# A GNN with mixture-of-experts layer on one Trainium2 core: more edges in the dense chunks, four late pairs, experts' weights loaded one expert at a time

## Chip, cores and metric

The kernel runs on one core of a Trainium2 chip. The metric is the device time of one execution in microseconds (us). The program is scheduled by hand: each engine (PE, the TensorE; DVE, the VectorE; ACT, the ScalarE; POOL, the GpSimd; SP, the SyncE, which here only issues DMAs) has its own instruction stream, and semaphores order them.

## What is computed

The input x has 6250 nodes of 256 features, with 206,250 edges sorted by target node. The reference, cut down:

```python
def gcn_layer(x, W, b):
    msg = (x @ W)[src] * norm[:, None]
    return relu(segment_sum(msg, dst, num_segments=6250) + b)

norm = edge_weight * rsqrt(deg_out[src] * deg_in[dst] + 1e-12)
h = gcn_layer(gcn_layer(layernorm(x), W6, b6), W7, b7)
x = x + h @ Wp + bp

xn = layernorm(layernorm(x)) * gamma + beta
top_vals, top_idx = top_k(xn @ Wr + br, 2)
w = softmax(top_vals)
for e in range(8):
    y += (gelu(xn @ W1[e] + b1[e]) @ W2[e] + b2[e]) * w_full[:, e]
x = x + y
```

Each expert has a W1 of 256 x 512 and a W2 of 512 x 256, float32.

## The kernel before

**Edges.** The edges form 202 groups of 8 tiles of 128 edges. They are summed in two ways. A *sparse* group is gathered: POOL issues 8 indirect DMAs (`gathers`, L912), each of which fetches 128 table rows; PE adds them per target node with 16 matmuls (`sums`, L2012) and one more (`combine`, L2024); ACT copies the sums out (`copy_sums` L1670, `copy_rows` L1677), and SP stores them to `zsum` in DRAM (`store_group`, L708). The ring of gathered groups has four places, so that POOL waits for the sums of the fourth group back. A *dense* tile is not gathered. DVE writes two one-hot matrices for it (`tile_one_hots`, L1218 and L1219), PE turns them into a piece of an adjacency matrix with three bf16 matmuls (`build_tile`, L1979), and DVE adds that to the adjacency of its chunk (`add_tile`, L1238). A *chunk* of `CT` = 30 tiles is then applied to the whole feature table in 27 steps of 98 matmuls in all (`apply_step`, L1992). The first 90 groups are dense in layer 1 (24 chunks, 720 tiles); two extra chunks of `LATE_CT` = 24 tiles make it 96 groups in layer 2.

**Layer 1.** A loop of 12 turns handles two chunks and 8 sparse groups in each: while PE builds the tiles of one chunk it applies the chunk before. SP stores each finished chunk to DRAM, for layer 2. After the loop a tail of `TAIL` = 16 turns sums the last 16 groups, builds the extra chunks (`EXTRAS`) and projects the pairs: a *pair* is 256 nodes, 25 in all, 23 of which come two or three a turn from turn 4 on (`TAIL_PAIRS`). For a pair SP loads its sums (`load_early`, which calls `load_pair`, L734, into `zrow`), DVE scales them (L1275), PE transposes them (L2033), ACT applies bias and relu (`pair_relu`, L1710, into `hT`), and PE projects them (L2050). The result is the feature table of layer 2, without which POOL can't gather there.

**Layer 2** runs in slots, one per sparse group. A chunk takes `SPANS[c]` slots: three for the first `SHORT` = 6, then four. On the first slot of a chunk SP issues the load of the chunk after it (`load_chunk`, L728). Each pair passes six stages in six successive slots: 0 scales, transposes and projects it; 1 adds the residual (DVE, L1287) and normalizes twice; 2 transposes (L2063) and takes the router's logits (L2073); 3 ranks the experts and adds the second bias, for which ACT copies eight weights per node (L1742) and PE multiplies (L2094), and SP stores the pair's rows (`rows_x`, L766) and its accumulator (`acc`, `store_acc`, L770); 4 and 5 place it in the experts' lists (one-hots by DVE, L1373; PE, L2112). `pair_from` says from which slot on a pair's sums are ready, and `pair_starts` makes the table `STARTS` from it, pairs at least three slots apart. The residual of a pair uses the same buffer as the accumulator store of the pair before. At the slot after the last chunk (`CHUNKS_END` = 98) ACT issues the loads of all experts' weights (`load_experts`, `load_weights`, L1817 and L1818): their place in SBUF is that of layer 1's table, free once the last chunk is applied.

**Experts.** From slot `GROUPS[1]` on, two blocks of 128 (token, expert) places run per slot, 105 in all. POOL gathers a block's rows (`take_block`, L923), PE and ACT run the two matmuls and gelu, ACT weights the result (`block_out`, L1797), and POOL adds it to `acc` in DRAM by an indirect DMA (`add_block`, L936). Blocks under `WHOLE` = 74 are formed from the lists of the first 22 pairs alone and their adds may go two in flight; from `WHOLE` on, where the `LATE_PAIRS` = 3 last started pairs come in, each add waits for the one before.

Of the kernel before, what the change touches and what calls it, by code (L numbers as in the profile page):

```python
# [6 lines left out]
BF16 = mybir.dt.bfloat16  # L7
# [35 lines left out]
GROUP_AT = [CT * h + 7 * s + 4 for h in range(2) for s in range(GPI // 2)]  # L43
# [8 lines left out]
BLOCKS, LATE_PAIRS, ZERO_PAIRS, PER_SLOT = 105, 3, 2, 2  # L52
# [29 lines left out]
def gnn_moe_kernel(nc, A):  # L82
# [36 lines left out]
    with ExitStack() as ctx:  # L119
# [43 lines left out]
        iota_b = sb("iota_b", [P, P], BF16)  # L163
# [7 lines left out]
        iota_col = sb("iota_col", [P, PLACES], BF16)  # L171
# [94 lines left out]
        col_n = area(o_a + 2 * P + KEYS, PLACES).bitcast(I32)  # L266
# [54 lines left out]
        trash = l2(PT)  # L321

# [111 lines left out]
        x_stored, hot_ready, list_mm = sem("x_stored"), sem("hot_ready"), sem("list_mm")  # L434
        list_closed, list_copied, last_row_made = sem("list_closed"), sem("list_copied"), sem("last_row_made")
# [77 lines left out]
        def chunk_slot(it, u):  # L513

            return 2 * it - 1 + u // CT, u % CT


        STEPS = CT - 3
# [6 lines left out]
        def group_at(it):  # L525

            return GROUP_AT if it else FIRST_GROUPS_AT

        def slice_bounds(i):
# [4 lines left out]
        TURNS = TAIL - TAIL_FROM - 2  # L534
        TAIL_PAIRS = [range(0)] * TAIL_FROM + [range(LATE_PAIR * k // TURNS, LATE_PAIR * (k + 1) // TURNS)
                                               for k in range(TURNS)] + [range(0)] * 2
# [14 lines left out]
        def chunk_start(c):  # L551
            return CT * min(c, CHUNKS) + LATE_CT * max(c - CHUNKS, 0)

        def chunk_of(t):
            return t // CT if t < DT else CHUNKS + (t - DT) // LATE_CT
# [5 lines left out]
        EXTRAS = [range(DT + LATE_CT * k // FIRST_EXTRA, DT + LATE_CT * (k + 1) // FIRST_EXTRA)  # L561
                  for k in range(FIRST_EXTRA)]
        EXTRAS += [range(DTA - LATE_CT + LATE_CT * k // 8, DTA - LATE_CT + LATE_CT * (k + 1) // 8) for k in range(8)]
# [21 lines left out]
        def chunks_for(b):  # L585
            return next(c for c in range(ALL) if chunk_start(c) >= tiles_before((b + 1) * PT * P) + CT // 2)
# [35 lines left out]
        assert [b for _, b in STARTS[-LATE_PAIRS:]] == [*MERGED_PAIRS, NPAIR - 2, NPAIR - 1]  # L622
        assert CHUNKS_END < LISTED_AT and COPIED_AT < GROUPS[1] and WHOLE % 2 == 0
# [29 lines left out]
        def _(sp):  # L653
# [108 lines left out]
            def store_x(i, b, slot):  # L762

                sp.wait_ge(wf_ready, i + 1)
                sp.wait_ge(rows_zeroed, 16 * 2 * PT * ZERO_PAIRS)
                sp.dma_start(pair_rows(rows_x, b), zx[:, slot]).then_inc(x_stored, 16)  # L766
# [6 lines left out]
            with sp.If(bad < 1):  # L773
# [6 lines left out]
                for it in range(LOOP_GROUPS // GPI):  # L780
                    for u in range(2 * CT):
# [114 lines left out]
        def _(pool):  # L896
# [3 lines left out]
            pool.iota(col_n, pattern=[[1, PLACES]], base=-(PLACES // 2), channel_multiplier=0).then_inc(iota_made, 1)  # L900
# [74 lines left out]
        def _(dve):  # L975
# [25 lines left out]
            dve.wait_ge(iota_made, 5)  # L1001
            dve.tensor_copy(iota_f[:, :], iota_i)
            dve.tensor_copy(iota_b[:, :], iota_i)
            dve.tensor_copy(iota_key[:, 0:KEYS], key_i)
            dve.tensor_copy(iota_col[:, :], col_n)
# [138 lines left out]
            spans = (0, DT, 0, CHUNKS, CT), (DT, DTA, CHUNKS, ALL, LATE_CT)  # L1144
# [5 lines left out]
            for q in range(QUARTERS):  # L1150
# [5 lines left out]
            dve.tensor_tensor(cseld[:, 1:CHUNKS + 1], tmin_f[:, CT:DT + CT:CT], tmin_f[:, 0:DT:CT], ALU.subtract)  # L1156
            step(dve.tensor_tensor(cseld[:, CHUNKS + 1:], tmin_f[:, DT + LATE_CT:DTA:LATE_CT],
                                   tmin_f[:, DT:DTA - LATE_CT:LATE_CT], ALU.subtract))
# [217 lines left out]

            def copy_list():
# [180 lines left out]
            with dve.If(bad < 1):  # L1558
# [5 lines left out]
                for it in range(LOOP_GROUPS // GPI):  # L1564
                    for u in range(2 * CT):
                        t = it * 2 * CT + u
# [19 lines left out]
                for k in range(TAIL):  # L1586
# [18 lines left out]
            with dve.Else():  # L1605
# [10 lines left out]
                slow_layer(1)  # L1616
                with dve.Fori(0, NPAIR - LATE_PAIRS) as b:
# [27 lines left out]
        def _(act):  # L1645
# [220 lines left out]
            with act.If(bad < 1):  # L1866
# [3 lines left out]
                for it in range(LOOP_GROUPS // GPI):  # L1870
                    for u in range(2 * CT):
# [10 lines left out]
                for k in range(TAIL):  # L1882
# [8 lines left out]
                    if k == FIRST_STORED_AT:  # L1891
                        act.wait_ge(added, DT + LATE_CT)
# [12 lines left out]
            with act.Else():  # L1905
# [19 lines left out]
                load_weights()  # L1925
# [19 lines left out]
        def _(pe):  # L1945
# [151 lines left out]
            def open_list():  # L2097
                pe.matmul(ps_list, no_part, iota_col[0:1, :], start=True, stop=False)
# [139 lines left out]
            with pe.If(bad < 1):  # L2238
                for t in range(len(ps_b)):
                    build_tile(t)  # L2240
                for it in range(LOOP_GROUPS // GPI):
                    for u in range(2 * CT):
                        t = it * 2 * CT + u
                        c, step = chunk_slot(it, u)
                        if c >= 0 and step < STEPS:
                            if step == 0:
                                pe.wait_ge(added, CT * (c + 1))
# [131 lines left out]
```

## Time and profile before

| | us |
|---|---|
| median of 3 runs | 3206.28 |
| lowest and highest run | 3199.44, 3208.09 |
| the profiled execution | 3203.64 |
| span of its trace | 3201.8 |
| PE busy | 2693.6 (84%) |
| POOL busy | 1988.3 (62%) |
| DVE busy | 1897.6 (59%) |
| ACT busy | 854.6 (27%) |

The mean granted clock of the profiled execution is 0.926 of full speed. In the trace, times count from the span's start; "idle ... <-X" or "[... <-X]" is the time the engine stood before an instruction, and what ended that time. "issue" means that it waited for nothing the trace shows. Layer 1's gathers start at 373.5 us; layer 2's run from 1573.67 to 2668; the experts' blocks end at 3170.7.

### The profile page before, as it was taken

What the parts mean: (1) busy time and instruction counts of PE and PEld (TensorE: products, weight loads), DVE (VectorE), ACT (ScalarE), POOL (GpSimd) and SP (SyncE); (2) the same over time, 40 slices, a digit from 0 to 9 for tenths busy, and PEclk for the clock granted to TensorE, in tenths of its full rate; (3) what the DMA queues carried; (4) which work ended last, traced back from release to release, by engine and by line L of the source; (5) the groups of instructions that cost most, each with busy time, mean ns of one, the idle gap of its engine ahead of it and who ended that gap; (6) DMA issues with size and microseconds to landing.
All of it is one profiled execution on the core that took longest, in us unless ns stands there. A gap on an engine that the chain in (4) does not pass through costs nothing. (4 is left out here: it accounts for less than half of the span.)

```text
span 3201.8 us, 53454 instructions
## 1 busy us (share of the span) xinstructions
PE 2693.6 (84%) x17249; PEld 2025.2 (63%) x17249; DVE 1897.6 (59%) x5981; ACT 854.6 (27%) x2004; POOL 1988.3 (62%) x1964
## 2 busy tenths in 40 slices
PE   4567489999999999987599999999888876899984
PEld 3456257666666666654477666666666643789974
DVE  9999878887878878764204445555354446622210
ACT  5677611111111111113200101111000001456542
POOL 0000277777777777777477777777777663467653
PEclk8699799999999999998899999999998885999997
DMA  4011355555655555558667667666766663344434
GB/s 127 0 30 34 119 189 191 191 187 178 196 196 195 195 195 193 195 165 279 219 200 259 223 221 228 217 219 225 234 194 198 211 225 82 65 68 70 73 56 112
DMA packets 196686, 532.68 MB, mean 166 GB/s; under 512 B 39708, under 2 KB 127412, under 8 KB 189652
## 3 DMA queue, kind: packets, MB, share of 16 engines
q0 software_dynamic: 103872, 256.67, 31.0%
q1 hardware_dynamic: 89828, 254.39, 21.8%
q10 hardware_dynamic: 2736, 18.48, 1.5%
q8 instruction: 133, 2.18, 0.3%
q14 instruction: 117, 0.96, 0.1%
HBM read 379.28 MB, written 156.50 MB: 167 GB/s over the span
## 5 line engine op out<-in xcount | busy, mean ns | idle before, releaser
L912 POOL DMA_INDIRECT arena<-table,src_i x1744 | 1699.1, 974 | 598.5 <-issue 526.4
L1992 PE MATMUL bank<-arena 128*128 128x257 f32 x4900 | 1238.6, 388 | 4.5 <-ACT zcd L1689 3.7
L1992 PEld LDWEIGHTS bank<-arena 128*128 128x128 f32 x4900 | 885.7, 192 | 217.8 <-issue 106.7
L1238 DVE TENSOR_TENSOR arena<-arena,bank 128x294 f32 x768 | 348.9, 454 | 227.5 <-PE bank L1979 154.9
L1979 PE MATMUL bank<-arena 128*128 128x294 bf16 x2304 | 418.3, 295 | 71.1 <-DVE arena L1238 37.7
L1979 PEld LDWEIGHTS bank<-arena 128*128 128x128 bf16 x2304 | 222.4, 99 | 227.9 <-DVE arena L1238 64.5
L1219 DVE SCALAR_TENSOR_TENSOR arena<-iota_f,arena 128x256 f32<-128x256 f32 x768 | 359.8, 469 | 0.0
L2012 PE MATMUL bank<-arena,s_all 128*32 128x257 f32 x3488 | 299.1, 412 | 46.7 <-DMA arena<-table,src_i 41.1
L936 POOL DMA_INDIRECT acc<-arena x105 | 179.5, 1709 | 155.6 <-ACT arena L1797 130.8
L1680 ACT COPY arena<-zero 128x2144 f32<-128x2144 f32 (+1 forms) x104 | 159.1, 1561 | 381.7 <-DMA chunks<-arena 248.7
L1951 PE MATMUL bank<-arena 128*128 128x150 bf16 x1616 | 149.0, 252 | 111.4 <-DVE arena L1068 75.8
L1670 ACT COPY zs<-bank 128x257 f32<-128x257 f32 x109 | 40.9, 375 | 738.8 <-PE bank L2012 738.8
L1218 DVE TENSOR_SCALAR arena<-iota_key,arena 128x294 bf16<-128x294 bf16 x768 | 235.1, 306 | 0.0
L1490 DVE COPY arena<-arena 128x1024 f32 x105 | 75.7, 729 | 268.0 <-PE bank L2197 254.2
L903 POOL PARTITION_ALL_REDUCE bad_all<-bad_f x1 | 0.4, 380 | 358.2 <-DVE bad_f L1209 358.2
L2206 PE MATMUL bank<-arena 128*128 x840 | 203.1, 384 | 17.4 <-ACT arena L1797 17.4
L1951 PEld LDWEIGHTS bank<-arena 128*128 128x128 bf16 x1616 | 129.6, 108 | 132.2 <-DVE arena L1068 110.7
L2012 PEld LDWEIGHTS bank<-arena,s_all 128*32 128x32 f32 x3488 | 122.0, 114 | 142.3 <-issue 50.8
L2197 PE MATMUL bank<-arena 128*128 128x128 f32 x1680 | 208.5, 278 | 0.0
L2197 PEld LDWEIGHTS bank<-arena 128*128 128x128 f32 x1680 | 199.9, 195 | 0.1
L2206 PEld LDWEIGHTS bank<-arena 128*128 128x128 f32 x840 | 152.0, 191 | 39.1 <-issue 21.5
L923 POOL DMA_INDIRECT arena<-rows_x,arena x105 | 108.0, 1028 | 65.9 <-DVE arena L1400 35.7
(241 smaller groups left out, 2780.1 us busy)
## 6 DMA issues: line engine op xcount, KB each, us to landing
chunks<-arena SPq DMA_DIRECT2D x25, 3283.0 KB
arena<-chunks SPq DMA_DIRECT2D x24, 3283.0 KB, 13.4
arena<-table,src_i POOLq DMA_INDIRECT x1744
zsum<-zc SPq DMA_DIRECT2D x109, 128.5 KB, 3.6
zrow<-zsum SPq DMA_DIRECT2D x50, 257.0 KB, 4.6
arena<-in_W ACTq DMA_DIRECT2D x16, 512.0 KB, 16.4
rows_x<-arena SPq DMA_DIRECT2D x25, 264.0 KB
arena<-chunks ACTq DMA_DIRECT2D x2, 3283.0 KB, 13.2
```

Source lines behind the costliest of these rows:

```text
L912: pool.indirect_dma_start(gat[:, r, j, 0:D], None, table[L], bass.IndirectOffsetOnAxis(ap=src_i[:, col:col + 1], axis=0)).then_inc(gathere ...
L936: pool.indirect_dma_start(acc, bass.IndirectOffsetOnAxis(ap=row_e[:, j:j + 1], axis=0), ye[:, j % 2], None, compute_op=ALU.add).then_inc(y ...
L1218: dve.tensor_scalar(ohk[:, r], iota_key[:, 0:KEYS], key[:, t:t + 1], None, ALU.is_equal)
L1219: dve.scalar_tensor_tensor(out=words[:, r], in0=bc_mid(iota_f[:, :], 2), scalar=lo_f[:, t:t + 1], in1=bc_in(w_words[:, t], P), op0=ALU.is_ ...
L1238: dve.tensor_tensor(win, win, ps_b[t % len(ps_b)].rearrange("p (h w) -> p h w", w=TW), ALU.add).then_inc(added, 1)
L1680: act.copy(adj[:, c % 2, first:last], zero[:, :].unsqueeze(2).broadcast_to([P, last - first, AWID])).then_inc(zeroed, 1)
L1951: last = pe.matmul(ps_do, oh_lo[:, r, j // TI, :, j % TI], whi[:, r, j // TI, :, :, j % TI].rearrange("p i n -> p (i n)"), start=False, st ...
L1979: last = pe.matmul(ps_b[t % len(ps_b)], halves[:, t % OH_RING, word, :, half], ohk[:, t % OH_RING], start=(i == 0), stop=(i == 2))
L1992: last = pe.matmul(ps_ap, adj[:, c % 2, h, 0:P], xp[:, h], start=(h == 0), stop=(h == XB_ALL - 1))
L2012: last = pe.matmul(ps_seg[q * WIN:(q + 1) * WIN, :], s_mat[:, r, q * HQ + j], gat[:, r, q * HQ + j], start=(j == 0 and not second), stop=( ...
L2197: last = pe.matmul(ps_h[j % 2][:, c], w1_e[:, j % W1_RING, k, c * P:(c + 1) * P], xeT[:, j % 2, k], start=(k == 0), stop=(k == KD - 1))
L2206: last = pe.matmul(ps_y, hs[:, j % 2, c], w2_of(e, c), start=(c == 0), stop=(c == HC - 1))
```

## The change

- The chunks' sizes become a list: 16 chunks of 31 tiles, 8 of 30, then extra chunks of 17 and 31 (before: 24 of 30, and 24, 24). Dense tiles in layer 1: 736 in place of 720; in layer 2: 784 in place of 768. So two groups fewer are gathered in each layer (110 and 104 in place of 112 and 106), and the tail has 14 turns in place of 16.
- Eight chunks of layer 2 take three slots in place of six; `CHUNKS_END` falls from 98 to 96, and the slots from 115 to 113.
- The four last started pairs are late in place of three: `WHOLE` falls from 74 to 70, and SP writes zeros to the rows of four pairs at the start (16 DMAs) in place of two (8).
- The weights are loaded one expert per slot in the eight slots from `CHUNKS_END` on, two DMAs each, in place of 16 at once.
- `iota_b` and `iota_col`, constants of the list, are made late in layer 1's tail (`list_constants`) in place of the start, and lie where other data is dead by then.

```diff
-CT = 30
-DT = CHUNKS * CT
-LATE_CHUNKS, LATE_CT, SHORT = 2, 24, 6
-ALL = CHUNKS + LATE_CHUNKS
-DTA = DT + LATE_CHUNKS * LATE_CT
+SIZES = [31] * 16 + [30] * 8 + [17, 31]
+ALL, SHORT = len(SIZES), 8
+DT, DTA = sum(SIZES[:CHUNKS]), sum(SIZES)
...
-BLOCKS, LATE_PAIRS, ZERO_PAIRS, PER_SLOT = 105, 3, 2, 2
+BLOCKS, LATE_PAIRS, PER_SLOT = 105, 4, 2
...
-        TURNS = TAIL - TAIL_FROM - 2
+        TURNS = TAIL - TAIL_FROM - 1
...
-            for t in range(NB - ZERO_PAIRS * PT, NB):
+            for t in [b * PT + t for _, b in STARTS[-LATE_PAIRS:] for t in range(PT)]:
...
+            def list_constants():
+                dve.tensor_copy(iota_b, iota_f[:, :])
+                for at in range(0, PLACES, P):
+                    n = min(P, PLACES - at)
+                    last = dve.tensor_scalar(iota_col[:, at:at + n], iota_f[:, 0:n], float(at - PLACES // 2), None, ALU.add)
+                last.then_inc(columns_made, 1)
...
+                    if k == TAIL - 2:
+                        list_constants()
...
                 if n == CHUNKS_END:
-                    load_experts()
+                    act.wait_ge(applied[1], SLICES * ALL)
+                if CHUNKS_END <= n < CHUNKS_END + NE:
+                    load_expert(n - CHUNKS_END)
...
-            def load_experts():
-                act.wait_ge(applied[1], SLICES * ALL)
-                load_weights()
-
-            def load_weights():
-                for e in range(NE):
-                    act.dma_start(w1_sb[:, e], A["W1"][:, e * KD * H:(e + 1) * KD * H]).then_inc(w1_in, 16)
-                    act.dma_start(w2_sb[:, e], A["W2"][:, e * HC * D:(e + 1) * HC * D]).then_inc(w2_in, 16)
+            def load_expert(e):
+                act.dma_start(w1_sb[:, e], A["W1"][:, e * KD * H:(e + 1) * KD * H]).then_inc(w1_in, 16)
+                act.dma_start(w2_sb[:, e], A["W2"][:, e * HC * D:(e + 1) * HC * D]).then_inc(w2_in, 16)
```

The table `STARTS`, slots in which the pairs start, comes out so: before 10, 14, 17, 22, 27, 32, 35, 40, 43, 48, 51, 56, 59, 64, 71, 74, 79, 82, 87, 90, 95, 98, 101, 106, 109; now 10, 13, 16, 20, 23, 30, 33, 38, 41, 46, 49, 54, 57, 62, 65, 70, 73, 78, 85, 88, 93, 96, 99, 104, 107. Chunks of four slots start on slots 18, 22, ... 94 before, on 24, 28, ... 92 now.

ACT, around the slot after the last chunk, before (`arena<-in_W` is a load of weights, the `COPY` of 8x256 the one for the second bias):

```order
L1731 ACTIVATE arena<-bank,cols 128x256 x2
L1677 COPY zc<-bank 128x257
L1737 ACTIVATE arena<-arena 128x2
L1817 DMA arena<-in_W 128x1024
L1818 DMA arena<-in_W 128x1024
...
L1818 DMA arena<-in_W 128x1024
L1742 COPY arena<-bank 8x256
L1710 ACTIVATE hT<-bank,cols 128x256 x2
```

and in the changed kernel:

```order
L1746 ACTIVATE arena<-bank,cols 128x256 x2
L1692 COPY zc<-bank 128x257
L1752 ACTIVATE arena<-arena 128x2
L1829 DMA arena<-in_W 128x1024
L1830 DMA arena<-in_W 128x1024
L1757 COPY arena<-bank 8x256
L1725 ACTIVATE hT<-bank,cols 128x256 x2
L1829 DMA arena<-in_W 128x1024
L1830 DMA arena<-in_W 128x1024
L1685 COPY zs<-bank 128x257
```

Sixteen loads stood ahead of the copy; now two do, and the others lie one pair a slot behind it.

SP in layer 2, before, at slot 74, where a chunk starts (`arena<-chunks` is the load of the next), a pair starts (`zrow`, `in_x`) and the pair of slot 71 is in stage 3 (`rows_x`, `acc`):

```order
L734 DMA zrow<-zsum 128x2x257
L760 DMA arena<-in_x 128x2x256
L711 TENSOR_LOAD bc_i
L711 ISA x2
L719 ISA
L719 DMA zsum<-zcd 128x257
L728 DMA arena<-chunks 128x6566
L766 DMA rows_x<-arena 128x2x264
L770 DMA acc<-arena 128x2x256
```

and in the changed kernel at slots 72 and 73, where the chunk and the pair start in turn:

```order
L723 DMA zsum<-zcd 128x257
L732 DMA arena<-chunks 128x6566
L738 DMA zrow<-zsum 128x2x257
L764 DMA arena<-in_x 128x2x256
L709 TENSOR_LOAD bg_i
L709 ISA x2
L712 ISA
L712 DMA zsum<-zc 128x257
L770 DMA rows_x<-arena 128x2x264
L774 DMA acc<-arena 128x2x256
```

The chunk's load moved from just ahead of the `acc` store to a slot ahead of it.

## Rows read from the trace of the kernel before

**Rows 1.** Costliest groups of the page: busy, mean ns of one, idle before.

```profile
L912 POOL DMA_INDIRECT arena<-table,src_i x1744 | 1699.1, 974 | 598.5 <-issue 526.4
...
L1979 PE MATMUL bank<-arena 128*128 128x294 bf16 x2304 | 418.3, 295 | 71.1 <-DVE arena L1238 37.7
```

**Rows 2.** Windows: PE, PEld, DVE, ACT, POOL busy, clock, DMA share, GB/s; dense loop.

```profile
560.00:720.00 160.00, 155.58 (x1016) 110.57 (x1013) 129.71 (x389) 30.83 (x36) 122.47 (x123) 1.00 0.59 189
```

**Rows 3.** Groups by line of PE from 415 to 1385, the dense loop.

```profile
L2012 PE MATMUL bank<-arena,s_all 128*32 128x257 f32 x1488 | 118.7, 388 | 17.5 <-DMA arena<-table,src_i 17.5
```

**Rows 4.** Timeline of POOL between the layers: start, duration, idle before.

```profile
1534.95 0.94 POOL L912 DMA_INDIRECT arena<-table,src_i  x1 [0.30 <-issue]
1573.67 0.94 POOL L912 DMA_INDIRECT arena<-table,src_i  x1 [37.78 <-DMA table<-arena]
```

**Rows 5.** Timeline of PE in layer 1's tail.

```profile
1461.50 2.86 PE L1979 MATMUL bank<-arena 128*128 128x294 bf16 x9 [6.31 <-DVE arena L1238]
...
1480.47 1.99 PE L2050 MATMUL bank<-w,hT 128*128 128x256 f32 x8 [0.93 <-ACT hT L1710]
...
1490.78 1.11 PE L2033 MATMUL bank<-ident,zr_all 128*128 128x128 f32 x4 [8.32 <-DVE zr_all L1275]
```

**Rows 6.** Windows of line L2012 alone, layer 2: PE, PEld, clock, DMA.

```profile
2060.00:2330.00 270.00, 38.12 (x448) 15.53 (x448) 0.95 0.71 226
2330.00:2610.00 280.00, 37.18 (x400) 14.79 (x400) 0.91 0.62 193
```

**Rows 7.** POOL late in layer 2: groups from 2470 to 2610; one timeline row.

```profile
L912 POOL DMA_INDIRECT arena<-table,src_i x102 | 97.1, 952 | 43.8 <-issue 29.8 <-PE bank L2012 14.0
...
2637.59 0.94 POOL L912 DMA_INDIRECT arena<-table,src_i  x1 [13.99 <-PE bank L2012]
```

**Rows 8.** Timeline of DVE, the residuals of pairs (L1287) in layer 2.

```profile
2047.75 0.69 DVE L1287 TENSOR_TENSOR arena<-bank,arena 128x512 f32<-128x512 f32 x1 [4.88 <-DMA acc<-arena]
...
2360.78 0.69 DVE L1287 TENSOR_TENSOR arena<-bank,arena 128x512 f32<-128x512 f32 x1 [11.10 <-DMA acc<-arena]
...
2540.73 0.69 DVE L1287 TENSOR_TENSOR arena<-bank,arena 128x512 f32<-128x512 f32 x1 [7.50 <-DMA acc<-arena]
```

**Rows 9.** Timeline of PE early in layer 2: apply matmuls back to back.

```profile
1719.57 4.95 PE L1992 MATMUL bank<-arena 128*128 128x257 f32 x22
```

**Rows 10.** Timeline of ACT and its queue at the weights' loads.

```profile
2607.71 0.36 ACTq L1817 DMA_DIRECT2D arena<-in_W  x1
...
2622.93 2.18 ACTq L1818 DMA_DIRECT2D arena<-in_W  x1
2625.21 0.36 ACT L1742 COPY arena<-bank 8x256 f32<-8x256 f32 x1 [17.31 <-issue]
```

**Rows 11.** Timeline of PE behind it.

```profile
2625.62 2.07 PE L2094 MATMUL bank<-arena 8*128 8x256 f32 x4 [15.33 <-ACT arena L1742]
...
2631.04 3.78 PE L2050 MATMUL bank<-arena,hT 128*128 128x256 f32 x8 [0.93 <-ACT hT L1710]
```

**Rows 12.** Windows ahead of the weights' loads and while they land (columns as in rows 2).

```profile
2560.00:2607.00 47.00, 44.97 (x266) 33.67 (x269) 22.92 (x101) 4.82 (x13) 33.16 (x35) 0.94 0.49 128
2617.00:2626.00 9.00, 0.38 (x1) 0.38 (x2) 0.00 (x0) 0.36 (x1) 5.08 (x6) 0.50 1.04 387
```

**Rows 13.** Timeline of ACT in the expert stage, ends of two blocks each.

```profile
2943.16 0.47 ACT L1797 ACTIVATE arena<-bank,arena 128x256 f32<-128x256 f32 x1 [0.58 <-PE bank L2206]
...
2946.91 0.48 ACT L1797 ACTIVATE arena<-bank,arena 128x256 f32<-128x256 f32 x1 [0.59 <-PE bank L2206]
...
3079.94 0.48 ACT L1797 ACTIVATE arena<-bank,arena 128x256 f32<-128x256 f32 x1 [2.65 <-DMA acc<-arena]
...
3084.56 0.48 ACT L1797 ACTIVATE arena<-bank,arena 128x256 f32<-128x256 f32 x1 [2.41 <-DMA acc<-arena]
```

More of the change, by code:

```diff
@@ L42 @@
 LOOP_GROUPS = 96
-GROUP_AT = [CT * h + 7 * s + 4 for h in range(2) for s in range(GPI // 2)]
+GROUP_AT = [7 * s + 4 for s in range(GPI // 2)]
 FIRST_GROUPS_AT = [5 * s + 18 for s in range(GPI)]
@@ L513, in chunk_slot, with tile_slots @@
         def chunk_slot(it, u):
-            return 2 * it - 1 + u // CT, u % CT
-        STEPS = CT - 3
+            first = SIZES[2 * it]
+            return (2 * it - 1, u) if u < first else (2 * it, u - first)
+        def tile_slots(it):
+            return range(SIZES[2 * it] + SIZES[2 * it + 1])
+        STEPS = 27
         ZERO_BEHIND = (8, 17, 25, STEPS - 1)
@@ L525, in group_at @@
         def group_at(it):
-            return GROUP_AT if it else FIRST_GROUPS_AT
+            return GROUP_AT + [SIZES[2 * it] + u for u in GROUP_AT] if it else FIRST_GROUPS_AT
         def slice_bounds(i):
@@ L551, in chunk_start @@
         def chunk_start(c):
-            return CT * min(c, CHUNKS) + LATE_CT * max(c - CHUNKS, 0)
+            return sum(SIZES[:c])
         def chunk_of(t):
-            return t // CT if t < DT else CHUNKS + (t - DT) // LATE_CT
+            return next(c for c in range(ALL) if t < chunk_start(c + 1))
         def group_no(L, n):
@@ L585, in chunks_for @@
         def chunks_for(b):
-            return next(c for c in range(ALL) if chunk_start(c) >= tiles_before((b + 1) * PT * P) + CT // 2)
+            return next(c for c in range(ALL) if chunk_start(c) >= tiles_before((b + 1) * PT * P) + 15)
         def groups_for(L, b):
@@ L621, in gnn_moe_kernel @@
         COPIED_AT = LISTED_AT + 3
-        assert [b for _, b in STARTS[-LATE_PAIRS:]] == [*MERGED_PAIRS, NPAIR - 2, NPAIR - 1]
-        assert CHUNKS_END < LISTED_AT and COPIED_AT < GROUPS[1] and WHOLE % 2 == 0
+        assert [b for _, b in STARTS[-LATE_PAIRS:]] == [NPAIR - 3, *MERGED_PAIRS, NPAIR - 2, NPAIR - 1]
+        assert CHUNKS_END <= LISTED_AT and CHUNKS_END + NE <= GROUPS[1] and COPIED_AT < GROUPS[1] and WHOLE % 2 == 0
         assert STARTS[-LATE_PAIRS][0] + 4 > COPIED_AT - 1
@@ L780, in _ @@
                 for it in range(LOOP_GROUPS // GPI):
-                    for u in range(2 * CT):
+                    for u in tile_slots(it):
                         c, step = chunk_slot(it, u)
@@ L1143, in _ @@
             dve.tensor_scalar(bg_i[:, :], tmin_f[:, ::2 * TG], float(ZROWS - P), None, ALU.min)
-            spans = (0, DT, 0, CHUNKS, CT), (DT, DTA, CHUNKS, ALL, LATE_CT)
+            turns = [c for c in range(ALL + 1) if c in (0, ALL) or SIZES[c] != SIZES[c - 1]]
+            spans = [(chunk_start(c0), chunk_start(c1), c0, c1, SIZES[c0]) for c0, c1 in zip(turns, turns[1:])]
             for t0, t1, c0, c1, n in spans:
@@ L1155, in _ @@
             dve.tensor_tensor(csel[:, 1:], tmin_f[:, 2 * TG::2 * TG], tmin_f[:, 0:-2 * TG:2 * TG], ALU.subtract)
-            dve.tensor_tensor(cseld[:, 1:CHUNKS + 1], tmin_f[:, CT:DT + CT:CT], tmin_f[:, 0:DT:CT], ALU.subtract)
-            step(dve.tensor_tensor(cseld[:, CHUNKS + 1:], tmin_f[:, DT + LATE_CT:DTA:LATE_CT],
-                                   tmin_f[:, DT:DTA - LATE_CT:LATE_CT], ALU.subtract))
+            for t0, t1, c0, c1, n in spans:
+                more = min(c1, ALL - 1) - c0
+                if more:
+                    last = dve.tensor_tensor(cseld[:, c0 + 1:c0 + more + 1], tmin_f[:, t0 + n:t0 + n * more + 1:n],
+                                             tmin_f[:, t0:t0 + n * more:n], ALU.subtract)
+            step(last)
             dve.tensor_scalar(off_i[:, :], dif[:, 0:DTA], 0.0, float(P), ALU.max, ALU.min)
@@ L1564, in _ @@
                 for it in range(LOOP_GROUPS // GPI):
-                    for u in range(2 * CT):
-                        t = it * 2 * CT + u
+                    for u in tile_slots(it):
+                        t = chunk_start(2 * it) + u
                         if t % LOADED == 0:
@@ L1616, in _ @@
                 slow_layer(1)
+                list_constants()
                 with dve.Fori(0, NPAIR - LATE_PAIRS) as b:
@@ L1870, in _ @@
                 for it in range(LOOP_GROUPS // GPI):
-                    for u in range(2 * CT):
+                    for u in tile_slots(it):
                         c, step = chunk_slot(it, u)
@@ L1924, in _ @@
                 act.wait_ge(p_stored, 16 * NPAIR)
-                load_weights()
+                for e in range(NE):
+                    load_expert(e)
                 with act.Fori(0, NPAIR) as b:
@@ L2241, in _ @@
                 for it in range(LOOP_GROUPS // GPI):
-                    for u in range(2 * CT):
-                        t = it * 2 * CT + u
+                    for u in tile_slots(it):
+                        t = chunk_start(2 * it) + u
                         c, step = chunk_slot(it, u)
```

26 lines of the change are left out of this document (13 added, 13 removed).

## The prediction

> **What bounds the kernel now.** I read the page first: its costliest group is POOL's gather, 1744 indirect DMAs with 1699.1 us busy, and all but 72 us of POOL's idle time before them is "issue" [rows 1]. The windows of the dense loop come next: in 160 us POOL starts 123 gathers, so 1.30 us each and 10.4 us for a group of 8, while PE is busy for 155.58 us of the 160 and DVE for 129.71 [rows 2]. Two engines are full at once there: PE waits for gathers only 17.5 us in 970 us of the loop [rows 3]. So shorter POOL work alone buys little, nor does shorter PE work. Third, the timeline of POOL: its last gather of layer 1 starts at 1534.95, the first of layer 2 at 1573.67, 38 us later [rows 4]. What fills these 38 us is the projection of the pairs: PE's timeline there shows it waiting for DVE (6.31 and 8.32 us) while POOL gathers on [rows 5]. In layer 2 the groups' sums (16 matmuls a group, one group a slot) tell which engine paces: 448/16 = 28 groups in 270 us is 9.6 us each, POOL's pace; 400/16 = 25 in the next 280 us is 11.2 us each, slower than POOL can go [rows 6]. PE paces from about 2330 on, and the waits of POOL for PE in [rows 7] agree.
>
> **The change, part by part.** *Sixteen tiles more in the chunks.* Two groups, 16 gathers, leave each layer. A tile costs PE three matmuls of 0.295 us [rows 1], 0.9 us: 16 x 0.9 = 14 us in layer 1. All sixteen lie in the loop, where PE's waits for gathers, 17.5 us, take them up; POOL still needs its 41.6 us for the four groups of a chunk. DVE has 30 us of 160 free [rows 2]. I take 0; if the waits don't come at the right chunks, up to +8. The two extra chunks stay 48 tiles together (17 and 31). Eight more zero fills at the start and the list's two constants, remade by five small DVE operations ahead of the last pairs, lie under other work: 0.
>
> *Layer 1's end.* POOL ends 16 x 1.30 = 20.8 us sooner. But the 23 pairs start once the last loop chunk is applied and cost PE 1.99 us of projection, 1.1 of transposes and 0.93 of waiting each [rows 5]; no gather of the group behind them is waited for there. The tail has two groups fewer to sum, about 2 x 1.7 us of PE work. I take -3, with ends 0 (pairs alone end the layer) and -21 (POOL does).
>
> *Layer 2.* 16 gathers of 1.25 us go: -20. From 2470 to 2610 POOL further waits 14.0 us for PE [rows 7]. Their cause, as I read it: where a pair starts three slots behind another on a chunk's first slot, SP issues the 3.3 MB chunk load just ahead of the acc store of the older pair, and DVE's residual of the younger one waits for that store, 11.10 us at the first and 7.50 at the last of three such places, against 4.88 where no load is ahead [rows 8]. In the new table of starts this falls on one slot (88) in place of three (74, 82, 90), so two thirds of the 14 us go: -9. Against it, slots 10 to 25 get fuller: five pairs start there (10, 13, 16, 20, 23) in place of four (10, 14, 17, 22), and chunks 6 and 7 have 3 slots in place of 4. A chunk of 98 apply matmuls at 4.95/22 us [rows 9] is 22 us of PE work; with three groups' sums (some 5 us) and one pair's (some 6 us) that is 33 us against POOL's 30. Over the five pairs that is 15 us of lag more, of which the ring of four groups (40 us of gathers) absorbs a part: +8, with ends 0 and +29 (all of it, at both places). Together -21, between -45 and +10.
>
> *The experts' weights.* Before, ACT issues all 16 loads of 512 KB in one go at slot 98, from 2607.71 to 2625.11. Its next copy waits 17.31 us, "issue" [rows 10], and PE, which needs that copy, stands for 15.33 us; its projection afterwards takes 3.78 us in place of 1.99 [rows 5, 11]. While PE stood, its granted clock was 0.50, the lower of its two levels (1.2 GHz), and the DMA engines were full, 387 GB/s [rows 12]. The change issues two loads in each of eight slots. Two take under 1 us where the queue is free (0.36 us for the first) [rows 10], and ACT is busy 4.82 us of 47 there [rows 12], so this hides. The transfers add 1.05 MB per 11 us, 95 GB/s, to the 128 that move in that stretch [rows 12]. I take -15.3 - 1.8 = -17, with ends 0 and -18. The row that speaks against the cover is POOL's wait for PE of 13.99 us at 2637.59 [rows 7]: it is the same stall, so not counted again. The Trainium skill ("DMA: Bandwidth & Descriptors", section "Issuing engines are not separate DMA queues") says that all issuers' DMAs run on the same 16 engines and interleave, and that the time to issue one "is usually small relative to the DMA itself". By it the stall would be the transfers' and spreading would save only the issue; the rows differ on the second half, since here issuing took 17.4 us of sequencer time that nothing could overtake, though the full engines are there too.
>
> *The expert stage.* WHOLE falls from 74 to 70: four more blocks whose scatter-add waits for the one before. Blocks with adds in pairs come 3.75 us apart (2943.16, 2946.91), serialized ones 4.62 (3079.94, 3084.56), with ACT waiting 2.4 us for the add [rows 13]: 4 x 0.87 = +3.5.
>
> **Sum:** 0 - 3 - 21 - 17 + 3.5 = -37.5. The profiled execution took 3203.64 us, 2.6 less than the median of 3206.28; with the sum it gives 3166, and the median 3169. I say 3167. About 0.3%, 9.6 us, is what a measurement of this kernel can tell from no change.
>
> **Rivals.** (1) *POOL ends layer 1 after all.* The pairs per turn are 2 or 3, with one turn more of the tail's fewer groups used; if the waits for DVE of 6.31 and 8.32 us [rows 5] shrink too, up to 18 us more go: 3149. For it: POOL and pairs end within 40 us of each other. Against: PE's sums follow the gathers by far there. (2) *The weights are bound by transfer.* They share the 16 engines with the gathers, and the last chunk's end is near. The 8.4 MB are 22 us at 387 GB/s; spread out they would stretch gathers, pair loads and acc stores in eight slots instead of one. If they give back all but 2 us, the sum is -22.5: 3182. The page of the Trainium skill named above leads here: by its section the transfers, not their issue, are what counts. (3) *The crowding eats layer 2's gain.* PE reaches the ring's limit in slots 10 to 25 and loses the 29 us at once, later recovering nothing: layer 2 is then -20 - 9 + 29 = 0, and the whole -16: 3188; worse by half that again and it is within 0.3%. (4) *Slower: PE paces all of layer 2.* If PE is at the ring's limit from slot 26 on, POOL's slack never comes back, and the pace of 11.2 us that PE keeps in the last 25 groups [rows 6] holds for the 45 slots before them as well. These ran at 10.05 (POOL); 45 x 1.15 = 52 us, and the -9 goes: 3166 + 52 + 9 = 3227, slower by 0.7%. It decides from the point where those slots take 10.9 us on the mean. For it: PE was busy 45 of 47 us in [rows 12] and paces already late; against it: 28 groups at 9.6 us in [rows 6], with the same 4-slot chunks and a pair every four slots, where PE kept up.
>
> **Chances.** Forecast 0.48, (1) 0.12, (2) 0.17, (3) 0.14, (4) 0.09. Faster by over 0.3%: the first three and a third of (3), 0.82. Within 0.3%: most of the rest of (3), 0.09. Slower: (4), 0.09. The range goes from (1) with some more, 3140, to just past (3), 3192; it leaves out (4) and part of (3).
>
> **What would show it.** Right: gathers x1712; no ACT copy behind 17 us of issue and no PE wait of 15 us for it near the last chunk's end, the clock there above 0.5; POOL's waits for PE late in layer 2 under 6 us in sum before the weights; layer 1's first table gather moved by only a few us; 35 blocks with acc waits. Wrong: the first gather of layer 2 some 20 us sooner (rival 1); waits for zrow, in_x or acc loads of 10 us in slots 96 to 103 (rival 2); POOL waiting for PE between slots 10 and 30 (rivals 3 and 4), and the groups' sums 11 us apart in the middle of layer 2 (rival 4). A loop chunk above 41.6 us would break the first zero.

## The result and the profile after

The changed kernel takes 3210.99 us (median of 20 runs) against 3205.4 us for the kernel before (20 runs): 1.0022 of it, with a 95% interval of 1.0013 to 1.0031. That is within 0.3%, no gain, where 3167 us was forecast. One execution of run 2 below took 6343.52 us and is left out of that run's numbers. The profiled execution took 3210.13 us, its span is 3208.3 us: 6.5 longer than before.

Four stretches show where it went. Each ends at an instruction that both traces have: the first gather of layer 2, the first sums of slot `CHUNKS_END`, the end of the first block, the end of the span.

| stretch, us | before | after | difference | forecast |
|---|---|---|---|---|
| to the first gather of layer 2 | 1573.7 | 1602.5 | +28.9 | -3 |
| from there to the sums of slot 98 (96) | 1033.2 | 998.8 | -34.4 | -21 |
| from there to the end of block 0 | 113.7 | 117.1 | +3.4 | -17 |
| from there to the end | 481.3 | 489.9 | +8.6 | +3.5 |

Groups of the page after: busy, mean ns of one, idle before. POOL's gathers fell by 32 as they should [rows 1]; its wait for the table grew from 40.8 to 55.7 us, and PE's wait for DVE ahead of its tiles from 37.7 us [rows 1] to 71.2.

```profile
L915 POOL DMA_INDIRECT arena<-table,src_i x1712 | 1673.3, 977 | 620.0 <-issue 514.9
...
L1992 PE MATMUL bank<-arena 128*128 128x294 bf16 x2352 | 428.8, 296 | 106.1 <-DVE arena L1243 71.2
```

The timeline of POOL between the layers (start, duration, idle before), where before had 37.78 us and 1573.67 [rows 4]:

```profile
1548.12 1.06 POOL L915 DMA_INDIRECT arena<-table,src_i  x1 [0.31 <-issue]
1602.55 0.94 POOL L915 DMA_INDIRECT arena<-table,src_i  x1 [53.37 <-DMA table<-arena]
```

**The loop of layer 1** is where the 28.9 us come from: the first tile of the first extra chunk is added at 1427.4, before at 1385.5, which is 41.9 us later. From there to layer 2's first gather the changed kernel takes 13.1 us less, 175.1 in place of 188.2. The groups of DVE by line, of the loop, of the kernel before and then of the changed one:

```profile
L1238 DVE TENSOR_TENSOR arena<-arena,bank 128x294 f32 x720 | 327.1, 454 | 201.9 <-PE bank L1979 139.7 <-issue 55.2 <-ACT arena L1680 4.3
```

```profile
L1243 DVE TENSOR_TENSOR arena<-arena,bank 128x294 f32 x736 | 334.4, 454 | 230.8 <-PE bank L1992 129.0 <-issue 96.1 <-ACT arena L1695 2.5
```

DVE's wait for PE did not grow (139.7 to 129.0 us), but "issue", time in which the trace shows nothing to wait for, has grown from 55.2 to 96.1 us. One such gap in the changed kernel's timeline, all engines, at the start of a chunk:

```profile
1291.17 0.43 SPq L727 DMA_DIRECT2D chunks<-arena  x1
...
1301.74 0.46 DVE L1243 TENSOR_TENSOR arena<-arena,bank 128x294 f32 x1 [8.39 <-issue]
...
1302.26 0.92 PE L1992 MATMUL bank<-arena 128*128 128x294 bf16 x3 [6.33 <-DVE arena L1243]
```

What DVE does in those 8.39 us stands in the view of line 1230 alone, in the window 1291 to 1303: `tile_offsets`, which loads the places of the next ten tiles from SBUF into DVE's registers.

```profile
L1230 DVEq TENSOR_LOAD <-off_i x1: 9499/9499/9499, 1292.0 to 1292.0; - x1
```

The next two loads of the chunk, begun 22 and 37 us behind its store, take 1.07 and 2.30 us (the same view, windows 1312 to 1316 and 1328 to 1332):

```profile
L1230 DVEq TENSOR_LOAD <-off_i x1: 1067/1067/1067, 1313.7 to 1313.7; - x1
...
L1230 DVEq TENSOR_LOAD <-off_i x1: 2300/2300/2300, 1328.5 to 1328.5; - x1
```

SP had issued the 3.3 MB store of the chunk just finished 0.8 us before the slow one; by the DMA view its queue moved the last of it some 11 us behind the issue. Loads come at every tenth tile of the whole count, so with chunks of 30 they fell on tiles 0, 10 and 20 of each: just ahead of the store and at its end. With 31 they drift by a tile a chunk, and from chunk 16 on stand at tiles 4, 14 and 24: one of the three inside the store.

**Layer 2** did what was forecast, and more: 400/16 = 25 groups in 250 us late in it, 10.0 us each, where before it took 280 [rows 6]. The windows of line L2025:

```profile
2330.00:2580.00 250.00, 34.12 (x400) 14.04 (x400) 0.95 0.68 221
```

**The weights' stall** of 15.33 us [rows 11] is gone. In its place PE waits for DVE, and DVE for a store (timelines of PE, DVE and SP):

```profile
2692.05 1.49 PE L2126 MATMUL bank<-off_i 128*128 128x400 bf16 x4 [22.70 <-DVE off_i L1378]
...
2678.43 0.69 DVE L1292 TENSOR_TENSOR arena<-bank,arena 128x512 f32<-128x512 f32 x1 [18.02 <-DMA acc<-arena]
...
2661.84 0.52 SPq L774 DMA_DIRECT2D acc<-arena  x1
```

From the accumulator's store's issue to the residual that waits for it 16.6 us pass here. ACT had issued the weights of two slots, 2.1 MB, from 2659.53 on, just ahead of it, and POOL's first six block gathers followed from 2663.91. In the kernel before, DVE's residual for the corresponding store (issued at 2666.50) began at 2674.24, 7.7 us later, without a wait: DVE was busy up to then, the most of it with the list of the whole blocks (2663.06 to 2672.08).

**The blocks** (ACT's wait for the scatter-add was 63.1 us in 26 blocks before; view of line 1814):

```profile
  DMA acc<-arena: 76.9, 32
```

### The profile page after: what moved, and what is told of

Read it like the earlier page. It is cut to its first block and busy times, and to the rows that moved or that the text cites. A ratio compares the mean times of both kernels' runs of the same rounds, so it can differ in the third digit from the quotient of the medians.

```text
span 3208.3 us, 53452 instructions
## 1 busy us (share of the span) xinstructions
PE 2691.9 (84%) x17225; PEld 2021.0 (63%) x17225; DVE 1907.2 (59%) x6031; ACT 853.8 (27%) x2000; POOL 1962.0 (61%) x1931
## 5 line engine op out<-in xcount | busy, mean ns | idle before, releaser
L915 POOL DMA_INDIRECT arena<-table,src_i x1712 | 1673.3, 977 | 620.0 <-issue 514.9
L1992 PE MATMUL bank<-arena 128*128 128x294 bf16 x2352 | 428.8, 296 | 106.1 <-DVE arena L1243 71.2
L1243 DVE TENSOR_TENSOR arena<-arena,bank 128x294 f32 x784 | 356.3, 454 | 247.1 <-PE bank L1992 135.9
L1224 DVE SCALAR_TENSOR_TENSOR arena<-iota_f,arena 128x256 f32<-128x256 f32 x784 | 369.1, 471 | 0.0
L2025 PE MATMUL bank<-arena,s_all 128*32 128x257 f32 x3424 | 294.3, 415 | 29.3 <-DMA arena<-table,src_i 23.9
L1964 PE MATMUL bank<-arena 128*128 128x150 bf16 x1616 | 149.7, 253 | 110.6 <-DVE arena L1069 76.1
L2025 PEld LDWEIGHTS bank<-arena,s_all 128*32 128x32 f32 x3424 | 119.4, 115 | 123.9 <-issue 51.4
L1665 ACT ACTIVATE arena<-iota_f,rel 128x128 bf16<-128x128 f32 x404 | 132.6, 427 | 39.8 <-PE bank L1964 39.6
```

Of the source, the lines that this page charges most:

```text
L915: pool.indirect_dma_start(gat[:, r, j, 0:D], None, table[L], bass.IndirectOffsetOnAxis(ap=src_i[:, col:col + 1], axis=0)).then_inc(gathere ...
L1224: dve.scalar_tensor_tensor(out=words[:, r], in0=bc_mid(iota_f[:, :], 2), scalar=lo_f[:, t:t + 1], in1=bc_in(w_words[:, t], P), op0=ALU.is_ ...
L1243: dve.tensor_tensor(win, win, ps_b[t % len(ps_b)].rearrange("p (h w) -> p h w", w=TW), ALU.add).then_inc(added, 1)
L1964: last = pe.matmul(ps_do, oh_lo[:, r, j // TI, :, j % TI], whi[:, r, j // TI, :, :, j % TI].rearrange("p i n -> p (i n)"), start=False, st ...
L1992: last = pe.matmul(ps_b[t % len(ps_b)], halves[:, t % OH_RING, word, :, half], ohk[:, t % OH_RING], start=(i == 0), stop=(i == 2))
L2025: last = pe.matmul(ps_seg[q * WIN:(q + 1) * WIN, :], s_mat[:, r, q * HQ + j], gat[:, r, q * HQ + j], start=(j == 0 and not second), stop=( ...
```

## The experiments

Two theories came out of this. O: the offsets' register loads are slow while a chunk's store runs, and the sizes of 31 moved them into it. W: the weights' spreading and the early list took away the cover under which the accumulator's store of slot 102 used to land. All ratios are to the kernel before, with 95% intervals.

**1. Offsets at fixed tiles of a chunk, in the changed kernel.**

```diff
+                at = [0, n - 20, n - 10] if n >= 30 else [0, 10]
...
-                        if t % LOADED == 0:
+                        if t == chunk_loads(t)[0]:
                             offs = tile_offsets(t)
-                        add_tile(t, offs[t % LOADED])
+                        add_tile(t, offs[t - chunk_loads(t)[0]])
```

> The changed kernel with one edit: DVE reads the tiles' offsets into its registers at a fixed place of each chunk (tiles 0, 11 and 21 of 31, or 0, 10 and 20 of 30) and not at every tenth tile of the whole count. Theory O (a register load that begins while the chunk ahead is being stored takes 3 to 9.5 us, and the sizes of 31 moved the loads into the store): loads beginning at tiles 2 to 9 are gone, a chunk of 30 or 31 takes 40.5 to 42 us, the loop ends some 25 to 30 us sooner than in the change, layer 2's first gather comes at 1570 to 1580 and not at 1602.5; time about 3182 to 3190, 0.993 to 0.996 of the kernel before. Rival P (sixteen more tiles simply make PE the bound of the loop): chunks still 44 us on the mean, first gather at 1600, time as the change, 1.002.

3185.04 us, 0.9934 (0.9921 to 0.9948). The loop took 1012.1 us (chunk 0 to chunk 24) in place of 1049.9, and layer 2's first gather came at 1580.5. DVE's groups by line, 415 to 1385, show the "issue" fallen:

```profile
L1250 DVE TENSOR_TENSOR arena<-arena,bank 128x294 f32 x704 | 320.2, 455 | 186.2 <-PE bank L1999 120.4 <-issue 63.6
```

Theory O held: 26 us of the change's time hung on these loads (their place, and with it the numbers that they start from, see run 5). Rival P, that the sixteen tiles are the cost, fell.

**2. The same place in the kernel before, which has no tile more.**

```diff
-                    off_i[0:1, t:min(t + LOADED, DTA)], [mybir.EngineType.DVE], min_val=0, max_val=P,
+                    off_i[0:1, t:min(t + LOADED if t else 4, DTA)], [mybir.EngineType.DVE], min_val=0, max_val=P,
...
-                        if t % LOADED == 0:
+                        if t == 0 or t % LOADED == 4:
                             offs = tile_offsets(t)
-                        add_tile(t, offs[t % LOADED])
+                        add_tile(t, offs[(t - 4) % LOADED if t > 3 else t])
```

> The kernel before with one edit: the offsets' register loads fall on tiles 4, 14 and 24 of each chunk, in place of 0, 10 and 20. No tile is added. Theory O: loads at tile 4 take 4 to 9 us, chunks 42 to 46 us, the loop 20 to 45 us longer, time 3225 to 3250, 1.006 to 1.014 of the kernel before. Rival P: nothing changes, 1.000.

3252.96 us (median of five), 1.0157 (1.0137 to 1.0176), somewhat more than expected. Groups of DVE by line, 415 to 1440:

```profile
L1238 DVE TENSOR_TENSOR arena<-arena,bank 128x294 f32 x685 | 311.5, 455 | 255.7 <-PE bank L1979 136.0 <-issue 116.0 <-ACT arena L1680 1.8
```

Moving the loads by four tiles, and nothing else, costs about 50 us: the loop takes 1065.7 us, 58 more, and the stretch from its end to layer 2's first gather 179.0, 9 less than the 188.2 before.

**3. Two experts a slot in four slots, in the changed kernel.**

```diff
-                if CHUNKS_END <= n < CHUNKS_END + NE:
-                    load_expert(n - CHUNKS_END)
+                if CHUNKS_END <= n < CHUNKS_END + NE // 2:
+                    for e in range(2 * (n - CHUNKS_END), 2 * (n - CHUNKS_END) + 2):
+                        load_expert(e)
```

> The changed kernel with the weights loaded two experts per slot in the four slots from the last chunk's end on, so that none is issued in slots 100 to 103. Theory W (the acc store of slot 102 lands late, 16.6 us after its issue, because the weights of slots 100 and 101 were issued 2 us ahead of it): DVE's wait for that store falls from 18.0 to under 9 us and the time by 8 to 10 us, to about 3201. Rival X (the six block gathers behind it, or the store alone, are what is slow): the wait stays at 15 us or more and the time is that of the change, 3211.

3208.13 us, 1.0013 (0.9999 to 1.0026). The wait fell to 7.80 us:

```profile
2675.20 0.69 DVE L1292 TENSOR_TENSOR arena<-bank,arena 128x512 f32<-128x512 f32 x1 [7.80 <-DMA acc<-arena]
```

The stretch to the end of block 0 fell from 117.1 to 110.6 us. So theory W held for the wait, and its gain is 6.5 us there, less than the 8 to 10 expected. In the total a gain isn't shown: the medians differ by 2.9 us and the two intervals overlap. The loop of layer 1 alone differs by more from one profiled execution to another (1049.9 us in the change, 1055.3 here).

**4. The kernel before with its weights spread, one expert a slot.**

```diff
                 if n == CHUNKS_END:
-                    load_experts()
+                    act.wait_ge(applied[1], SLICES * ALL)
+                if CHUNKS_END <= n < CHUNKS_END + NE:
+                    load_expert(n - CHUNKS_END)
...
```

> The kernel before with the weights loaded one expert per slot from slot 98 on, nothing else. The forecast's step: PE's stall of 15.3 us goes and with it 15 to 17 us, 3189, 0.995. Theory W: the stall goes, but the weights of later slots then stand ahead of an acc store; list_whole still hides 9 us of it, so 5 to 12 us are left, 0.996 to 0.9985. Rival Y (the pairs' chain of slots 98 to 105 sets the end and absorbs any stall): no gain, 0.999 to 1.001.

3199.91 us, 0.998 (0.9964 to 0.9995). The stretch to the end of block 0 fell from 113.7 to 105.0 us: 8.7 us for a stall of 15.3. Part of it comes back in waits for the lists, as this row of PE's timeline shows (8.32 before at that place):

```profile
2683.61 1.49 PE L2117 MATMUL bank<-off_i 128*128 128x400 bf16 x4 [12.34 <-DVE off_i L1373]
```

Within theory W's range; the forecast's step of 15 to 17 us is not.

**5. Two loads a chunk, at tiles 0 and 15**, in the changed kernel (the edit against run 1).

```diff
-                at = [0, n - 20, n - 10] if n >= 30 else [0, 10]
+                at = [0, n // 2] if n >= 30 else [0]
```

> As the run with the loads at fixed tiles, but two loads a chunk in place of three, at tiles 0 and 15, of 15 or 16 values each. Theory O: the load at tile 10 or 11, which still met the end of the store, is gone; no load over 3 us but a few; the loop (first tile of chunk 0 to the first of chunk 24) falls from 1012 to 1000 to 1008 us, time 3172 to 3182, 0.990 to 0.994. Rival Q (longer loads cost as much as they save, or POOL's 41.6 us a chunk sets the pace by now): loop 1012 again, 3185.

3235.46 us, 1.0094 (1.0072 to 1.0116): a miss for theory O and for its rival alike; no load had been expected to depend on where it starts. The view of the loads' line (min/median/max ns):

```profile
L1237 DVEq TENSOR_LOAD <-off_i x51: 1111/3604/8770, 372.4 to 1547.1; - x51
```

Sorted by their first tile, the loads of 16 values clear of a store take 1.1 us where that tile's number divides by 4 and 3.6 where it doesn't. Those of 15 values begun 2 us ahead of a store take 1.5 and 5.3 to 6.6. The traces of the two kernels had it too: ten values clear of a store take 1.06 us from a number that divides by 4, and 2.30 from the others. In the changed kernel the slowest loads (9.2 to 9.5 us) all start at numbers that don't; those that do and fall in the same place take 1.2 to 4.4.

**6. Three late pairs in the changed kernel.**

```diff
-BLOCKS, LATE_PAIRS, PER_SLOT = 105, 4, 2
+BLOCKS, LATE_PAIRS, PER_SLOT = 105, 3, 2
...
```

> The changed kernel with three late pairs in place of four: WHOLE is 74 again, and the list of whole blocks is made three slots after the last chunk, as in the kernel before, not at once. Theory W (the late list was cover: while DVE made it, the acc store landed, and POOL's first block gathers stayed out of the store's way): DVE's wait for the acc store falls from 18 to under 9 us, the serialized blocks cost 4 to 6 us less, time 3195 to 3202, 0.997 to 0.999. Rival X (the weights alone delay the store): the wait stays at 13 us or more, only the blocks' 4 to 6 us are gained, 3205 to 3207.

3198.39 us, 0.9972 (0.9957 to 0.9987), 12.6 us under the change. The row of DVE's timeline that had 18.02:

```profile
2667.29 0.69 DVE L1292 TENSOR_TENSOR arena<-bank,arena 128x512 f32<-128x512 f32 x1 [4.70 <-DMA acc<-arena]
```

The stretch to the end of block 0 is 106.3 us (117.1 in the change), the last 483.4 (489.9): 10.8 and 6.5 us. Rival X, by which only the blocks would gain, fell. Runs 3 and 6 together say that the store is late when the weights and the absence of the list's cover meet; mending either brings most of it back. In run 3 the store is quick, 6.6 us from its issue (2668.59) to the residual. In run 6 it still takes 12.7 (issued at 2654.63, as close behind 2.1 MB of weights), and the list hides most of that. POOL's first block gathers start behind it there, so at most the 3.9 us between 16.6 and 12.7 can be theirs; no run moves them alone.

**7. All weights at once in the changed kernel.**

```diff
-                if CHUNKS_END <= n < CHUNKS_END + NE:
-                    load_expert(n - CHUNKS_END)
+                if n == CHUNKS_END:
+                    for e in range(NE):
+                        load_expert(e)
```

> The changed kernel with all weights loaded at once at the last chunk's end, as before. The forecast's step: PE's stall of 15 us comes back and the time is 15 to 17 us longer, 3227. Theory W: the stall comes back, but the wait of 18 us for the acc store falls under 9, so that 3 to 8 us are lost, 3214 to 3219, 1.003 to 1.005.

3214.52 us, 1.0032 (1.0016 to 1.0048), 3.5 us over the change. The stall is back, and DVE's wait for the store is 8.19 us in place of 18.02 (7.2 from the store's issue); the stretch to block 0 is 116.8 us, as with the spreading:

```profile
2620.17 2.07 PE L2108 MATMUL bank<-arena 8*128 8x256 f32 x4 [11.76 <-ACT arena L1757]
```

So in this change the spreading is worth about nothing, not 17 us.

**8. The three mends together** (runs 5, 3 and 6).

> All three mends together: offsets loaded at tiles 0 and 15, weights two experts a slot, three late pairs. Theories O and W: what the single edits gain adds up, 3211 - 30 to 38 (loads) - 6 to 10 (acc store) - 4 to 6 (blocks), 3157 to 3172, 0.985 to 0.990. Rival (the gains overlap in the chain of slots 96 to 103): 3172 to 3180.

3218.02 us, 1.0033 (1.0021 to 1.0045): missed, because of run 5's loads. It is 17.4 us under run 5, where runs 6 and 3 alone gained 12.6 and 2.9; that run 3's part comes on top of run 6's isn't shown, and run 12 speaks against it.

**9. Loads of 12 or 16 values from tiles that divide by 4**, the last such at or ahead of a chunk's first tile and the one 16 behind it, in the changed kernel.

```diff
+            OFFS_AT = sorted({s for c in range(ALL) for s in (chunk_start(c) // 4 * 4, chunk_start(c) // 4 * 4 + 16) if s < DTA})
...
-                        if t % LOADED == 0:
+                        if t in OFFS_AT:
                             offs = tile_offsets(t)
-                        add_tile(t, offs[t % LOADED])
+                        add_tile(t, offs[t - max(s for s in OFFS_AT if s <= t)])
```

> The changed kernel, with the offsets loaded 12 or 16 at a time from tiles whose number divides by 4, the last such at or before a chunk's first tile and the one 16 after it. Theory O, with what the run with halves showed (a load from a number that divides by 4 takes 1.1 to 1.6 us, one from another number 2.3 us for 10 values, 3.6 for 15, and up to 6 where the store begins behind it): no load over 2.5 us, the loop at 995 to 1008 us, time 3168 to 3182, 0.988 to 0.993. Rival R (it is the number of values that costs, not where they start): loads of 3.5 to 6 us at the chunks' starts, time 3225 to 3240.

3180.51 us, 0.9912 (0.9889 to 0.9935). No load is over 1.32 us, and "issue" ahead of DVE's adds (415 to 1385) all but goes:

```profile
L1233 DVEq TENSOR_LOAD <-off_i x51: 848/1099/1320, 372.1 to 1494.2; - x51
```

```profile
L1246 DVE TENSOR_TENSOR arena<-arena,bank 128x294 f32 x701 | 320.0, 457 | 180.2 <-PE bank L1995 174.6 <-issue 2.3
```

The loop took 1009.0 us, a little over the expected 995 to 1008: it keeps POOL's pace now, for in that window PE waits 33.7 us for gathers and 2.8 for DVE's adds. Rival R, that the number of values costs, fell. All these loads both start at a number that divides by 4 and begin ahead of a store or 13 us and more behind its issue; what each of the two is worth in time was not separated.

**10. The same loads in the kernel before.**

> The kernel before with the same loads. Theory O: its loads of 2.3 to 4.7 us go as well; PE's share of the loop shrinks, but POOL's 10.4 us a group hold the pace, so that 0 to 8 us are gained, 3198 to 3206. Rival: the loads set the pace of the kernel before too, 10 to 25 us gained, under 3195.

3199.46 us, 0.9972 (0.996 to 0.9984): as expected, 6 us. The kernel before lost little to these loads, by the place that its chunks of 30 give them.

**11. Fitted loads and three late pairs.**

> The run with fitted loads and three late pairs. Theories O and W add up: 12 to 13 us below the run with fitted loads, 3156 to 3170, 0.984 to 0.989. Rival (the gains overlap): less than 6 us below it.

3163.25 us, 0.986 (0.9835 to 0.9885). The gains add up: 17.3 us below run 9, where 12 to 13 were expected. This beats both kernels, by 42 us and 48.

**12. The same with two experts a slot.**

> As the run before it, with two experts a slot in four slots. Theory W: with the late list as cover the acc store is waited for by under 5 us already, so there is nothing left for it to gain, within 4 us of the run before it. Rival X (the weights hold up more than that store): 5 to 10 us better.

3162.27 us, 0.9859 (0.9831 to 0.9887): no difference from run 11, as theory W has it.

**13. The store moved, first try.** In the changed kernel SP's `store_chunk` was put at step 12 of the next chunk.

```diff
-                        if step == 0 and c >= 0:
+                        if step == 12 and c >= 0:
                             store_chunk(c)
```

> The changed kernel with each chunk's store issued by SP at step 12 of the next chunk and not at step 0; the offsets' loads stay where the change has them. Theory O-store (the store is what slows a register load that begins within about 10 us behind it): loads at tiles 1 to 9 of a chunk take 1.1 to 2.5 us, loads at tiles 11 to 19 now up to 7 to 9.5. Rival S (something else at a chunk's start, as the tiles without apply work there, or the groups' sums, slows them): the loads over 3 us stay at tiles 2 to 9 and those at 11 to 19 stay at 1.1 or 2.3.

3210.98 us, 1.0006 (0.999 to 1.0021): it tells nothing. SP isn't bound to PE's steps; it runs ahead to its next wait, and the store still began 0.8 us ahead of the load at tile 4.

**14. The store held back by a wait.**

```diff
-                sp.wait_ge(added, chunk_start(c + 1))
+                sp.wait_ge(added, chunk_start(c + 1) + (12 if c < CHUNKS - 1 else 0))
```

> The changed kernel with SP waiting for twelve tiles more before it issues a chunk's store, so that the store really begins at tile 12 of the next chunk (in the run before, only its place among SP's instructions moved, and the store began when it had before). Theory O-store: the loads at tiles 1 to 9 take 1.06 or 2.3 us, those at tiles 12 to 19 up to 9.5; time within 15 us of the change. Rival S (something else at a chunk's start): the loads over 3 us stay at tiles 2 to 9, those at 12 to 19 stay at 1.06 or 2.3.

In the loop the loads at tiles 1 to 9 now take 1.1 to 2.4 us (one 2.7), those at 12 to 18 up to 9.2. One chunk: its store by the timeline of SP's queue, and the load that met it (view of line 1230, 1077 to 1090).

```profile
1077.04 0.34 SPq L727 DMA_DIRECT2D chunks<-arena  x1
```

```profile
L1230 DVEq TENSOR_LOAD <-off_i x1: 5829/5829/5829, 1082.8 to 1082.8; - x1
```

So it is the store that slows them; rival S fell. The expected time was missed by far: 3335.42 us, 1.0406 (1.0383 to 1.0429), because ACT, which clears the buffer behind the store, waits for it (the waits of ACT, 420 to 1430):

```profile
ACT arena L1695 <- DMA chunks<-arena: 509.7, 20, 27.7
```

## Why the prediction was wrong

**"Sixteen tiles more: 0, if the waits don't come at the right chunks, up to +8."** This step failed. The loop became 42 us longer (1007.5 to 1049.9). The sixteen tiles themselves were priced right: with the loads put right the loop of 736 tiles takes 1009.0 us (run 9), that of 720 1005.7 (run 10), 3.3 less. (PE's waits for gathers were a little more than the 17.5 us of [rows 3]: line L2009 has 3.8 more in the same view.) What the step left out is an instruction that the view of groups doesn't list: the offsets' register load, of which the page shows only the "issue" ahead of L1238. Its cost hangs on where a chunk's boundaries fall, and the change moves those. The prediction counted DVE's 30 us of room in 160 [rows 2] as cover, but a load of 9.5 us in one piece is longer than what PE has in hand: it built three more tiles and then stood for 6.33 us. Of the 55.2 us of "issue" in the loop before, the prediction said nothing; it was the sign that something there took time, as were the 37.7 us for which PE waited for DVE's adds [rows 1].

**"Layer 1's end: -3."** From the first extra chunk's first tile to layer 2's first gather the change took 175.1 us, the kernel before 188.2: 13 us less, where -3 was taken. That is not the step's worth. With the loads put right in both kernels the stretch is the same, 184.5 us (run 9) and 184.6 (run 10): the term is 0, the end "pairs alone end the layer". A loop held up by loads shortens it, as run 2 shows with no tile more (179.0), so part of the loop's loss comes back here.

**"Layer 2: -21."** It gave -34.4 with the two slots fewer counted in. With the loads put right it is -30.0 (run 9 against run 10). The signs that were forecast came: the pace late in the layer went from 11.2 to 10.0 us a group, and POOL no longer waits for PE from 2470 on; the crowding showed, as a wait of POOL for PE of 12.8 us between 1800 and 1900, where +8 was put in. Late in the layer three of DVE's residuals waited more than 6 us for an accumulator's store before (11.10, 7.79 and 7.50); now one does ahead of slot 96 (6.68). That these collisions are what the gain beyond the forecast comes from is likely and not shown: no run changes the starts or the chunks' sizes of layer 2 alone.

**"The weights: -17."** This step failed too: +3.4 in that stretch. The stall went, but behind it stood another that DVE's list had covered before, and the transfers lay ahead of a store that the pairs' chain needs. The prediction moved the list and called it nothing; that the 9 us of list-making were cover for a store was not looked for. Even in the kernel before, where the list stayed, spreading gave 8.7 us there (run 4), not 17. Of rival 2, weights bound by their transfer, the place and the sign held, the size didn't. The Trainium skill ("DMA: Bandwidth & Descriptors", section "Issuing engines are not separate DMA queues") has all issuers' DMAs interleave on the same engines; the trace agrees, an accumulator's store of SP needing 16.6 us behind 2.1 MB that ACT had issued, and 6.6 where they were out of its way (run 3).

**"The expert stage: +3.5."** It was +8.6: six blocks more waited, not four, and ACT's waits for adds rose by 13.8 us. Run 6 gives 6.5 of it back.

Of the rivals, none named the register loads. The line "a loop chunk above 41.6 us would break the first zero" was the test that failed: chunks took 43.7 us on the mean. But it was set at POOL's pace and not at the kernel before, whose chunks already took 42.0. Run 11, the change with three late pairs and without the loads' cost, came out at 3163, near the forecast of 3167. That is in part luck: against the kernel before its layer 2 gained 30.3 us, not 21, and its weights' stretch 6.5, not 17.

## What to carry to other kernels

"Issue" time in front of an engine's instruction can be work of its sequencer, here register loads, and belongs in the sum like any other; when sizes change, see where such loads fall against large transfers. A step that is moved off a queue may have been the cover for a transfer, so ask of each moved step not only what it costs, but what lands while it runs. Where a stall is removed, look for the second-latest of the waits at that place, because that is all that can be gained.

## What the runs showed of the hardware

A register load of ten values from SBUF on DVE took 1.06 us from a first value whose number divides by 4 and 2.30 from another, as long as no large store ran; of 16 values, 1.1 and 3.6. Four, eight and twelve values from a number that divides by 4 took 0.37 us (the last load of the change), 0.60 (the last of the kernel before) and 0.85 (run 9). So, as an estimate from these figures, such a load costs some 0.25 us for every four values, and another 0.23 for every one. The Trainium skill ("Runtime: NRT & Kernel Launch", section "Instruction fetch mechanics") gives about 200 ns a register for loads from HBM; 2.30 us for ten is near that, 1.06 half of it, and these came from SBUF. Begun within some 10 us behind the start of a 3.3 MB store from SBUF the same loads of ten took up to 9.7 us (run 7) from a number that doesn't divide by 4 and up to 4.4 from one that does; run 14 moved the store and the slow loads moved with it.
